# Second attention: the low half of the queries made by VectorE from the PSUM bank, one index copy a batch

## The chip, the core and the metric

The program runs on one NeuronCore of a Trainium2 chip. Its engines are TensorE (PE in the profile, with PEld for its weight loads), VectorE (DVE), ScalarE (ACT), GpSimd (POOL) and SyncE (SP), which here only starts DMAs. Each engine runs its own instructions in the order in which they were written and waits on semaphores. The metric is the device time of one launch in microseconds (us). Three runs of the kernel before took 2513.68, 2516.06 and 2517.75 us, median 2516.06.

## The reference, cut to what matters

The model is a cross attention, a mixture of experts, a second cross attention and a feed-forward layer, for 16 batches of 256 tokens of width 256. The change touches the second attention (16 heads of 64) and the gather of the expert results that stands ahead of it.

```
x = x + tanh(g_ffn[0]) * _L0_ffn_ref(_layernorm(x), ...)          # two experts a token, plus a shared one
x = x + tanh(g_xattn[1]) * _L1_xattn_ref(_layernorm(x), ctx, ctx, mask, ...)

q = split_heads(Q @ W_q + b_q)                                     # Q = _layernorm(x)
k = split_heads(K @ W_k + b_k)                                     # K = V = ctx
v = split_heads(V @ W_v + b_v)
scores = einsum('bhqd,bhkd->bhqk', q, k) / sqrt(d)                 # d = 64
scores = where(mask == 0, -1e9, scores)
probs = softmax(scores, axis=-1)
out = einsum('bhqk,bhkd->bhqd', probs, v)
return out.reshape(...) @ W_o + b_o
```

## The kernel before, in words

The second attention is the function `attention1`. Every float32 matrix is carried as a high and a low half in float16, and a product is three matmuls (high by high, high by low, low by high). So each projected result has to be split: high = float16(value), low = float16(value - high).

A batch has 16 units; unit u is the pair of heads u // 2 for one half of the query rows. The work is a pipeline over batches, written as 16 turns a batch. In a turn TensorE computes the scores of unit u (L1023 to L1027, into one of two banks `pS`), transposes the probabilities of unit u - 3 (L1035), in each even turn multiplies a pair of heads by the values (L1048) and projects an older pair (L1060), and then computes a piece of the next batch's front. VectorE in a turn takes the negative row maximum of the scores (L1212), the inverse of the row sums of unit u - 1 (L1216), the low half of the transposed probabilities (L1222), in even turns the low half of the output (L1227), and then its share of the next batch's front. ScalarE in a turn makes the high half of the transposed probabilities (L1121), in even turns the high half of the output (L1126), then the two exponentials (L1112), then its share of the front. GpSimd in a turn scales the probabilities of unit u - 1 by the inverse sums (L941, "normalise"), then its share of the front, then a gather.

The front of the next batch has three stretches, given by the lists KEYS, QUERIES and VALUES: key chunks on TensorE in turns 2 to 6, query chunks in turns 7, 8, 8, 9, 10, 10, 11, 12, value chunks in turns 12 to 17 (16 and 17 are turns 0 and 1 of the step after). Two banks `pF` serve them in rotation; a chunk waits until the bank's reader two chunks earlier is done. Before the change the path of the four query chunks is: TensorE fills a bank, ScalarE writes the value with bias and the factor 1/8 as float32 to `q32` (L1094, turns 8, 9, 10, 12) and thereby frees the bank, GpSimd casts it to float16 (L923) and subtracts (L925), SyncE starts the DMAs that stack the halves into `QS` (L878, L879), which the scores of the next batch read. Keys go the same way, except that VectorE (L1198) writes the float32 value. Value chunks are read by ScalarE (L1103) and then VectorE (L1205), straight from the bank.

The combine step (`comb`) works two batches ahead: in turns 1, 3, 7 and 11 GpSimd copies a column of row numbers into a small tile (L898) and starts an indirect DMA that gathers 128 rows (L901); in turns 4, 6, 10 and 13 VectorE adds the gathered rows to X (L1153), after every second one it takes row statistics (L1157). GpSimd computes the inverse root (L907), VectorE refines it (L1170 to L1173), and the result `rstd` scales the normalised input `xn` (L1183), which only the queries use.

Of the kernel before, what the change touches and what calls it, by code (L numbers as in the profile page):

```python
# [10 lines left out]
U32 = mybir.dt.uint32  # L11
# [724 lines left out]
def attention1(nc, ctx, X, XW, ctxT_d, mask_d, bias_d, consts, POS, GW, y_d):  # L736
# [7 lines left out]
    UNITS = 2 * PAIRS  # L744
    LIFT = 4096.0
    MASKED = -2.0 ** 40
    QS = [[s.sb(f"QS{i}{a}", [P, PAIRS, S], F16) for a in range(2)] for i in range(2)]
# [14 lines left out]
    maskq = [s.sb(f"maskq{i}", [P, 2, S], BF16) for i in range(2)]  # L762
    k32, q32 = [s.sb(f"k32{i}", [P, 2, S]) for i in range(2)], [s.sb(f"q32{i}", [P, 2, S]) for i in range(2)]
    QN, KN = [s.sb(f"QN{i}", [P, PAIRS, S], F16) for i in range(2)], [s.sb(f"KN{i}", [P, PAIRS, S], F16) for i in range(2)]
# [5 lines left out]
    proj = s.sb("proj", [P, 2, D])  # L770
    pick = [[s.sb(f"pick{i}{q}", [P, 1], U32) for q in range(2 * TOPK)] for i in range(2)]
    routed = [[s.sb(f"routed{i}{q}", [P, D]) for q in range(2 * TOPK)] for i in range(2)]
# [15 lines left out]
    f_full = s.counter("f_full", 13)  # L788
    pick_ready, gathered = s.counter("pick_ready", 4), [[s.counter(f"gathered{i}{q}", 16, start=0) for q in range(4)] for i in range(2)]
    combined, var_ready, root_ready = s.counter("combined", 4), s.counter("var_ready", 1), s.counter("root_ready", 1)  # L790
    comb_steps = s.chain("comb_steps", 7)
    k_flat, q_flat = s.counter("k_flat", 4), s.counter("q_flat", 4)
    qk_high, qk_split = s.counter("qk_high", 8), s.counter("qk_split", 8)
    stacked = [s.counter(f"stacked{half}", 160) for half in range(2)]
# [55 lines left out]
    with nc.Block() as block:  # L850
        @block.sync
        def _(sp):
# [7 lines left out]
            def stack(b, par):  # L860
# [4 lines left out]
                for half in range(2):  # L865
                    qk_split.wait(sp, b, 2 * half + 2)
                    pr = slice(4 * half, 4 * half + 4)
                    for a in range(2):
                        r = slice(64 * a, 64 * a + 64)
                        sp.dma_start(KD2[par][a][0:64, pr, :], KN[0][r, pr, :]).then_inc(stacked[half].sem, 16)  # L870
                        sp.dma_start(KD2[par][a][64:P, pr, :], KN[0][r, pr, :]).then_inc(stacked[half].sem, 16)
                        sp.dma_start(KZ[par][a][0:64, pr, :], KN[1][r, pr, :]).then_inc(stacked[half].sem, 16)
                for half in range(2):
                    qk_split.wait(sp, b, 4 + 2 * half + 2)
                    pr = slice(4 * half, 4 * half + 4)
# [10 lines left out]
        def _(pool):  # L886
# [6 lines left out]
            def comb(b, par, turn):  # L893
                def gather(q):
                    j, k = q // TOPK, q % TOPK
                    if not isinstance(b, int) or b > 1:
                        combined.wait(pool, b, q - 2 * TOPK * 2 + 1)
                    nc.gpsimd.tensor_copy(pick[par][q][:], POS[:, k, bass.ds(2 * b + j, 1)]).then_inc(pick_ready.sem, 1)  # L898
                    pick_ready.wait(pool, b, q + 1)
                    nc.gpsimd.nop(nofuse=True)  # L900
                    nc.gpsimd.indirect_dma_start(out=routed[par][q][:], out_offset=None, in_=y_d,  # L901
                                                 in_offset=bass.IndirectOffsetOnAxis(ap=pick[par][q][:], axis=0)).then_inc(gathered[par][q].sem, 16)

# [6 lines left out]
            def front(b, par):  # L910
# [3 lines left out]

                def split(n):

                    q = n % 4
                    pr = slice(2 * q, 2 * q + 2)
                    dst, src, flat = ((KN, k32, k_flat), (QN, q32, q_flat))[n // 4]
                    flat.wait(pool, b, q + 1)  # L920
                    stacked[q // 2].wait(pool, b, 0)
                    nc.gpsimd.nop(nofuse=True)
                    nc.gpsimd.tensor_copy(dst[0][:, pr, :], src[q % 2][:]).then_inc(qk_high.sem, 1)  # L923
                    qk_high.wait(pool, b, n + 1)
                    nc.gpsimd.tensor_tensor(dst[1][:, pr, :], src[q % 2][:], dst[0][:, pr, :], ALU.subtract).then_inc(qk_split.sem, 1)  # L925

                def make_mask():
# [4 lines left out]
                return plan((0, context_low), (MASK, make_mask),  # L932
                            *[(KEYS[2 * q + 1], lambda q=q: split(q)) for q in range(4)],
                            *[(QUERIES[2 * q + 1], lambda q=q: split(4 + q)) for q in range(4)])

# [11 lines left out]
        def _(pe):  # L947
# [10 lines left out]
            def front(b, par):  # L958
# [29 lines left out]
                def queries(q, a):  # L988
                    if a == 0:
                        if q < 2:  # L990
                            k_flat.wait(pe, b, 3 + q)
                        else:
                            q_flat.wait(pe, b, q - 1)
                    chunk(5 + q, Wv["q"], xh, xl, q, a)

                def values(n, kt):
                    j, half = n // 2, n % 2
                    if kt == 0:
                        if n < 2:
                            q_flat.wait(pe, b, 3 + n)  # L1000
                        else:
# [69 lines left out]
        def _(act):  # L1071
# [5 lines left out]
            def front(b, par):  # L1077
# [55 lines left out]
        def _(dve):  # L1133
# [7 lines left out]
            def comb(b, par, turn):  # L1141
# [35 lines left out]
            def front(b, par):  # L1177
# [14 lines left out]
                def keys(q):  # L1192

                    f_full.wait(dve, b, 2 + q)
                    qk_split.wait(dve, b, q - 1 if q > 1 else -4) if q > 1 or not isinstance(b, int) or b else None
                    for a in range(2):
                        p2 = 2 * q + a
                        last = nc.vector.tensor_scalar(k32[q % 2][:, a, :], pF[(1 + q + par) % 2][:, a * S:(a + 1) * S], bqk[:, 1, p2:p2 + 1], None, ALU.add)  # L1198
                    last.then_inc(k_flat.sem, 1)

                def values(n):
# [1067 lines left out]
```

## Time and profile before

| what | value |
|---|---|
| median of three runs | 2516.06 us |
| the profiled execution, own time | 2506.78 us |
| its span, first to last instruction | 2504.8 us |
| span of the second attention | about 1418 to 2300 us of it |
| one batch of it in the steady state | 52.0 us (L1183 at 1516.36, 1568.36) |
| mean granted clock of TensorE, whole span | 0.916 |

Times are microseconds; "idle before" is the time in which the engine had nothing to run before an instruction, with what ended it. A name such as `a_pT` is a tile of an attention with its buffer number left out. The rows with a time ahead give start, duration, engine, line, operation, output and inputs, and in brackets the idle time before it. An instruction can overlap the tail of the one ahead of it on its engine.

### The profile page before, as it was taken

To read this page: it belongs to the slowest core of one execution; us is meant where nothing else is said; L and a number is where in the kernel's file an instruction comes from. 1 tells how busy PE (TensorE), PEld (TensorE's weight loads), DVE (VectorE), ACT (ScalarE), POOL (GpSimd) and SP (SyncE) were. 2 spreads that over 40 slices of the span, in tenths; PEclk is the share of its full clock that TensorE was granted. 3 is DMA by queue.
4 is the path that set the end of the run, shared out by engine and by line. 5 is a ranking of instruction groups with operands and counts; after the bars stand their busy time and mean duration, and the time that the engine had idled before them with its cause. 6 is when DMAs were issued, how large, how long until landed. Compare 5 with 4: busy or idle time off the path is not lost. (4 is left out here: it accounts for less than half of the span.)

```text
span 2504.8 us, 48924 instructions
## 1 busy us (share of the span) xinstructions
PE 1948.7 (78%) x14975; PEld 1386.5 (55%) x14984; DVE 1609.6 (64%) x3340; ACT 1111.6 (44%) x2557; POOL 876.2 (35%) x1363
## 2 busy tenths in 40 slices
PE   1798988988904597099999679898998889994275
PEld 1576676766603364066666456676666667673122
DVE  5777777877567543044444357777777777776797
ACT  1354444544434122022222146666666666673363
POOL 2000000000000243322332377777776777762004
PEclk9899999999955799599999899999999999997598
DMA  3000000000043000012221133223222232321001
GB/s 101 9 5 8 8 4 8 8 4 4 1 160 128 7 0 1 25 54 66 70 73 57 47 97 79 61 64 83 74 71 70 62 75 74 75 56 36 0 0 67
DMA packets 91507, 118.61 MB, mean 47 GB/s; under 512 B 18264, under 2 KB 60904, under 8 KB 91368
## 3 DMA queue, kind: packets, MB, share of 16 engines
q1 hardware_dynamic: 80872, 94.74, 13.8%
q0 software_dynamic: 8576, 17.87, 2.7%
q10 hardware_dynamic: 1920, 4.19, 0.5%
q8 instruction: 81, 1.33, 0.2%
q14 instruction: 58, 0.48, 0.1%
HBM read 56.92 MB, written 17.90 MB: 30 GB/s over the span
## 5 line engine op out<-in xcount | busy, mean ns | idle before, releaser
L1112 ACT ACTIVATE a_P<-a_pS,a_NM 128x256 f32<-128x256 f32 x512 | 237.2, 470 | 158.1 <-DVE a_NM L1212 157.8
L941 POOL TENSOR_SCALAR a_P<-a_P,a_RS 128x256 f32<-128x256 f32 x512 | 255.3, 499 | 113.2 <-DVE a_RS L1216 75.6
L504 PE MATMUL a_pT<-a_Q,a_K 128*128 128x256 f32 x1024 | 243.0, 383 | 8.6 <-ACT a_PT L587 8.6
L1212 DVE TENSOR_REDUCE a_NM<-a_pS 128x2 f32<-128x512 f32 x256 | 175.5, 686 | 96.6 <-PE a_pS L1027 95.0
L587 ACT ACTIVATE a_PT<-a_pT 128x512 f32<-128x512 f32 x256 | 151.2, 597 | 187.5 <-PE a_pT L504 187.1
L420 POOL TENSOR_TENSOR a_cl<-a_ctxin,a_ch 128x512 f16<-128x512 f32 x16 | 18.6, 1160 | 542.5 <-ACT a_ch L557 542.5
L504 PEld LDWEIGHTS a_pT<-a_Q,a_K 128*128 128x128 f32 x1024 | 183.6, 190 | 38.8 <-ACT a_PT L587 16.5
L1222 DVE TENSOR_TENSOR a_PL<-a_pT,a_PH 128x512 f16<-128x512 f32 x256 | 173.6, 678 | 48.2 <-ACT a_PH L1121 48.0
L1121 ACT ACTIVATE a_PH<-a_pT 128x512 f16<-128x512 f32 x256 | 153.1, 598 | 110.0 <-PE a_pT L1035 95.5
L1035 PE MATMUL a_pT<-g_ident,a_P 128*128 128x128 f32 x1024 | 157.9, 277 | 43.8 <-POOL a_P L941 34.8
L694 DVE TENSOR_REDUCE a_M<-a_pS 128x2 f32<-128x512 f32 x256 | 162.8, 682 | 32.8 <-PE a_pS L483 32.2
L1035 PEld LDWEIGHTS a_pT<-g_ident,a_P 128*128 128x128 f32 x1024 | 117.4, 141 | 74.9 <-POOL a_P L941 52.4
L1027 PE MATMUL a_pS<-a_KZ,a_QS 128*128 128x256 f16 x512 | 125.9, 273 | 0.0
L1026 PE MATMUL a_pS<-a_KD,a_QS 128*128 128x256 f16 x512 | 125.8, 273 | 0.0
L1707 ACT ACTIVATE me_hh<-me_pH 128x512 f16<-128x512 f32 x72 | 43.0, 597 | 175.7 <-PE me_pH L1692 175.7
L99 PE MATMUL a_pF<-a_ch,xw_XW 128*128 128x256 f16 x512 | 98.3, 276 | 27.2 <-DVE a_VL L1205 23.1
L1756 DVE TENSOR_TENSOR me_h<-me_SG,me_pU 128x512 f32<-128x512 f32 x72 | 49.5, 687 | 98.5 <-PE me_pU L99 98.5
L1705 ACT ACTIVATE me_SG<-me_pG 128x512 f32<-128x512 f32 x72 | 43.0, 597 | 147.8 <-PE me_pG L99 147.8
L99 PE MATMUL me_pG<-mo_w1h,me_xt 128*128 x288 | 98.7, 384 | 6.9 <-issue 6.9
L1112 ACT ACTIVATION_READ_ACCUMULATOR a_P<-a_pS,a_NM 128x1 f32 x512 | 102.8, 201 | 0.0
L99 PE MATMUL a_pF<-a_xh,xw_XW 128*128 128x256 f16 x512 | 98.9, 273 | 2.4 <-DVE a_k L1198 2.4
L1023 PE MATMUL a_pS<-a_maskq,g_identb 128*128 128x512 bf16 x256 | 97.4, 380 | 2.9 <-POOL a_maskq L931 2.4
(410 smaller groups left out, 5507.5 us busy)
## 6 DMA issues: line engine op xcount, KB each, us to landing
a_KD<-a_KN SPq DMA_DIRECT2D x128, 128.0 KB
a_QS<-a_QN SPq DMA_DIRECT2D x128, 128.0 KB
we_stage<-mw SPq DMA_DIRECT2D x24, 512.0 KB, 4.7
ys<-me_yb SPq DMA_DIRECT2D x72, 128.0 KB, 1.7
a_ctxin<-ctxT SPq DMA_DIRECT2D x32, 256.0 KB, 2.8
a_KZ<-a_KN SPq DMA_DIRECT2D x64, 128.0 KB
g_X<-x SPq DMA_DIRECT2D x1, 4096.0 KB, 15.0
rows<-mr_row SPq DMA_DIRECT2D x32, 128.0 KB, 1.7
```

The source lines that it names most:

```text
L99: last = nc.tensor.matmul(out, a(kt), b(kt), start=(n == 0), stop=(n == 3 * chunks - 1))
L504: last = nc.tensor.matmul(pT[h % 2][:, kt, :], K32[par][h % 2][:, h // 2, kt * P:(kt + 1) * P], Q32[par][:, h // 2, :], start=True, stop=True)
L587: nc.scalar.activation(PT[h % 8][:], pT[h % 2][:], ACT.Exp, scale=float(dh) ** -0.5).then_inc(p_ready.sem, 1)
L694: nc.vector.reduce_max(M[:, k % 2, k - k % 2:k - k % 2 + 2], pS[k % 2][:], AX.X).then_inc(s_max.sem, 1)
L941: last = nc.gpsimd.tensor_scalar(P32[u % 4][:, a, :], P32[u % 4][:, a, :], RS[u % 4][:, a:a + 1], LIFT, ALU.mult, ALU.mult)
L1026: nc.tensor.matmul(out[:, a, :], q, KD2[par][a][:, p2, :], start=False, stop=False)
L1027: last = nc.tensor.matmul(out[:, a, :], q, KZ[par][a][:, p2, :], start=False, stop=(a == 1))
L1035: last = nc.tensor.transpose(pT[u % 2][:, a, kt, :], P32[u % 4][:, a, kt * P:(kt + 1) * P], ident[:])
L1112: last = nc.scalar.activation(P32[u % 4][:, a, :], pS[u % 2][:, a, :], ACT.Exp, bias=NM[u % 4][:, a:a + 1], accum_out=SM[u % 4][:, a:a + 1])
L1121: nc.scalar.activation(PH[p2 % 2][:, :, :, j * P:(j + 1) * P].rearrange("p a k q -> p (a k) q"), pT[u % 2][:].rearrange("p a k q -> p (a k ...
L1212: nc.vector.tensor_reduce(NM[u % 4][:], pS[u % 2][:], AX.X, ALU.max, negate=True).then_inc(s_max.sem, 1)
L1222: nc.vector.tensor_tensor(PL[p2 % 2][:, :, :, j * P:(j + 1) * P].rearrange(f), pT[u % 2][:].rearrange(f), PH[p2 % 2][:, :, :, j * P:(j + 1 ...
```

## The change

Queries are no longer written as float32. ScalarE reads the bank and writes the float16 high half directly; VectorE then reads the same bank, adds the bias, subtracts the high half and writes the low half; only then is the bank free. GpSimd's cast and subtract remain for the keys alone. The factor 1/8 leaves ScalarE's instruction and goes into the two constants with which `rstd` is refined. The four index copies of a batch become one, into a tile of four columns. The counters that keys and queries shared are parted.

```
     def gather(q):
         ...
-        nc.gpsimd.tensor_copy(pick[par][q][:], POS[:, k, bass.ds(2 * b + j, 1)]).then_inc(pick_ready.sem, 1)
-        pick_ready.wait(pool, b, q + 1)
+        if q == 0:
+            nc.gpsimd.tensor_copy(pick[par][:], POS[:, :, bass.ds(2 * b, 2)]).then_inc(pick_ready.sem, 1)
+            pick_ready.wait(pool, b, 1)
         nc.gpsimd.nop(nofuse=True)
         nc.gpsimd.indirect_dma_start(out=routed[par][q][:], out_offset=None, in_=y_d,
-                                     in_offset=bass.IndirectOffsetOnAxis(ap=pick[par][q][:], axis=0))...
+                                     in_offset=bass.IndirectOffsetOnAxis(ap=pick[par][:, k, j:j + 1], axis=0))...
...
-    def split(n):
-        q = n % 4
+    def split(q):
         pr = slice(2 * q, 2 * q + 2)
-        dst, src, flat = ((KN, k32, k_flat), (QN, q32, q_flat))[n // 4]
-        flat.wait(pool, b, q + 1)
+        k_flat.wait(pool, b, q + 1)
         stacked[q // 2].wait(pool, b, 0)
         nc.gpsimd.nop(nofuse=True)
...
-                *[(QUERIES[2 * q + 1], lambda q=q: split(4 + q)) for q in range(4)])      # GpSimd
...
     def queries(q, a):                                                                    # TensorE
...
-                q_flat.wait(pe, b, q - 1)
+                q_lo.wait(pe, b, q - 1)
...
     def queries(q):                                                                       # ScalarE
         f_full.wait(act, b, 6 + q)
-        qk_split.wait(act, b, 3 + q if q > 1 else 0) if q > 1 or not isinstance(b, int) or b else None
+        stacked[q // 2].wait(act, b, 0)
         for a in range(2):
             p2 = 2 * q + a
-            last = nc.scalar.activation(q32[q % 2][:, a, :], pF[(5 + q + par) % 2][:, a * S:(a + 1) * S], ACT.Identity,
-                                        bias=bqk[:, 0, p2:p2 + 1], scale=float(dh) ** -0.5)
-        last.then_inc(q_flat.sem, 1)
+            last = nc.scalar.activation(QN[0][:, p2, :], pF[(5 + q + par) % 2][:, a * S:(a + 1) * S], ACT.Identity, bias=bqk[:, 0, p2:p2 + 1])
+        last.then_inc(q_hi.sem, 1)
...
+    def queries(q):                                                                       # VectorE
+        q_hi.wait(dve, b, q + 1)
+        for a in range(2):
+            p2 = 2 * q + a
+            last = nc.vector.scalar_tensor_tensor(QN[1][:, p2, :], pF[(5 + q + par) % 2][:, a * S:(a + 1) * S], bqk[:, 0, p2:p2 + 1],
+                                                  QN[0][:, p2, :], ALU.add, ALU.subtract)
+        last.then_inc(q_lo.sem, 1)
...
-        link(nc.vector.tensor_scalar(corr[:], corr[:], -0.5, 1.5, ALU.mult, ALU.add))
+        link(nc.vector.tensor_scalar(corr[:], corr[:], SHRINK * -0.5, SHRINK * 1.5, ALU.mult, ALU.add))    # SHRINK = dh ** -0.5
```

SyncE's wait ahead of the query DMAs is on `q_lo` in place of `qk_split`, TensorE's first two value chunks wait on `q_lo` in place of `q_flat`. No DMA is added or taken away.

On VectorE, turns 8 to 10 of a step before the change (`a1_NM` is written by the maximum, `a1_RS` by the inverse, `a1_PL` by the low half of the probabilities, `a1_ol` by that of the output):

```order
L1212 TENSOR_REDUCE a1_NM0<-a1_pS0 128x2
L1216 RECIPROCAL a1_RS3<-a1_SM3 128x2
L1222 TENSOR_TENSOR a1_PL0<-a1_pT1,a1_PH0 128x4x128
L35 REGISTER_ALU
L1227 SCALAR_TENSOR_TENSOR a1_ol1<-a1_pO,a1_oh1 128x256
L35 REGISTER_ALU
L1212 TENSOR_REDUCE a1_NM1<-a1_pS1 128x2
L1216 RECIPROCAL a1_RS0<-a1_SM0 128x2
L1222 TENSOR_TENSOR a1_PL1<-a1_pT0,a1_PH1 128x4x128
L35 REGISTER_ALU
```

The same place in the changed kernel, where the lines of the maximum, the inverse and the low half are L1218, L1222 and L1228:

```order
L1218 TENSOR_REDUCE a1_NM0<-a1_pS0 128x2
L1222 RECIPROCAL a1_RS3<-a1_SM3 128x2
L1228 TENSOR_TENSOR a1_PL0<-a1_pT1,a1_PH0 128x4x128
L35 REGISTER_ALU
L1233 SCALAR_TENSOR_TENSOR a1_ol1<-a1_pO,a1_oh1 128x256
L1202 SCALAR_TENSOR_TENSOR a1_QN1<-a1_pF1,a1_bqk,a1_QN0 128x256 x2
L35 REGISTER_ALU
L1218 TENSOR_REDUCE a1_NM1<-a1_pS1 128x2
L1222 RECIPROCAL a1_RS0<-a1_SM0 128x2
L1228 TENSOR_TENSOR a1_PL1<-a1_pT0,a1_PH1 128x4x128
L1202 SCALAR_TENSOR_TENSOR a1_QN1<-a1_pF0,a1_bqk,a1_QN0 128x256 x2
```

A pair of instructions on the query bank (L1202) now stands between the work of one turn and the maximum of the turn after it, in turns 8, 9, 10 and 12.

On GpSimd, turns 7 to 10 of a step before the change (`a1_P32` are the probabilities that it normalises):

```order
L898 COPY a1_pick12<-g_POS 128x1
L35 REGISTER_ALU
L901 DMA a1_routed12<-ys,a1_pick12 128x256
L35 REGISTER_ALU
L941 TENSOR_SCALAR a1_P323<-a1_P323,a1_RS3 128x256 x2
L923 CAST a1_QN0<-a1_q320 128x512
L35 REGISTER_ALU
L925 TENSOR_TENSOR a1_QN1<-a1_q320,a1_QN0 128x512
L35 REGISTER_ALU
L941 TENSOR_SCALAR a1_P320<-a1_P320,a1_RS0 128x256 x2
L923 CAST a1_QN0<-a1_q321 128x512
```

The same place in the changed kernel:

```order
L903 DMA a1_routed02<-ys,a1_pick0 128x256
L35 REGISTER_ALU
L940 TENSOR_SCALAR a1_P323<-a1_P323,a1_RS3 128x256 x2
L35 REGISTER_ALU
L940 TENSOR_SCALAR a1_P320<-a1_P320,a1_RS0 128x256 x2
L35 REGISTER_ALU
L940 TENSOR_SCALAR a1_P321<-a1_P321,a1_RS1 128x256 x2
L35 REGISTER_ALU
L940 TENSOR_SCALAR a1_P322<-a1_P322,a1_RS2 128x256 x2
```

The copy ahead of the gather and every cast and subtract between two normalisations are gone from these turns.

## Rows read from the trace of the kernel before

**Rows 1.** One batch: busy us (count) of PE, PEld, DVE, ACT, POOL; clock, DMA share, GB/s.

```profile
1983.00:2035.00 52.00, 47.30 (x414) 35.54 (x413) 38.58 (x87) 33.24 (x103) 39.00 (x60) 1.00 0.29 72
```

**Rows 2.** Waits of TensorE, 1588 to 2185 us: total, times, longest.

```profile
PE a_pT L1035 <- POOL a_P L941: 26.0, 54, 1.8
```

**Rows 3.** TensorE in order of time, one batch: start us, us, instruction [idle before].

```profile
1642.64 0.66 PE L1035 MATMUL a_pT<-g_ident,a_P 128*128 128x128 f32 x4 [0.55 <-POOL a_P L941]
...
1644.44 0.38 PE L1060 MATMUL a_pG<-xw_XW,a_oh 128*128 128x256 f16 x2 [0.36 <-DVE a_proj L1231]
...
1667.96 0.66 PE L1035 MATMUL a_pT<-g_ident,a_P 128*128 128x128 f32 x4 [1.01 <-POOL a_P L941]
...
1678.39 0.28 PE L99 MATMUL a_pF<-a_ch,xw_XW 128*128 128x256 f16 x1 [1.49 <-DVE a_VL L1205]
```

**Rows 4.** GpSimd in order of time, the same batch.

```profile
1640.26 1.16 POOL L925 TENSOR_TENSOR a_KN<-a_k,a_KN 128x512 f16<-128x512 f32 x1
...
1646.18 0.18 POOL L898 COPY a_pick<-g_POS 128x1 uint32 x1
...
1648.26 1.03 POOL L941 TENSOR_SCALAR a_P<-a_P,a_RS 128x256 f32<-128x256 f32 x2
1649.35 0.61 POOL L923 CAST a_QN<-a_q 128x512 f16<-128x512 f32 x1
...
1651.30 1.12 POOL L941 TENSOR_SCALAR a_P<-a_P,a_RS 128x256 f32<-128x256 f32 x2
...
1662.43 1.16 POOL L925 TENSOR_TENSOR a_QN<-a_q,a_QN 128x512 f16<-128x512 f32 x1
```

**Rows 5.** GpSimd, an indirect DMA that follows another, in the expert stage.

```profile
850.84 0.96 POOL L1527 DMA_INDIRECT slots<-st_val,st_idx  x1 [0.30 <-issue]
```

**Rows 6.** VectorE in order of time, the same batch as rows 3.

```profile
1640.62 1.08 DVE L1153 SCALAR_TENSOR_TENSOR g_X<-a_routed,g_GW,g_X 128x256 f32 x1
...
1645.14 0.68 DVE L1212 TENSOR_REDUCE a_NM<-a_pS 128x2 f32<-128x512 f32 x1
...
1646.40 0.41 DVE L1227 SCALAR_TENSOR_TENSOR a_ol<-a_pO,a_oh 128x256 f16<-128x256 f32 x1
...
1651.60 0.47 DVE L1153 SCALAR_TENSOR_TENSOR g_X<-a_routed,g_GW,g_X 128x256 f32 x1
...
1662.77 1.10 DVE L1153 SCALAR_TENSOR_TENSOR g_X<-a_routed,g_GW,g_X 128x256 f32 x1
...
1664.88 0.69 DVE L1212 TENSOR_REDUCE a_NM<-a_pS 128x2 f32<-128x512 f32 x1
...
1667.75 0.68 DVE L1212 TENSOR_REDUCE a_NM<-a_pS 128x2 f32<-128x512 f32 x1
...
1670.85 0.69 DVE L1212 TENSOR_REDUCE a_NM<-a_pS 128x2 f32<-128x512 f32 x1 [0.78 <-PE a_pS L1027]
```

**Rows 7.** ScalarE in order of time, the same batch.

```profile
1643.98 0.59 ACT L1121 ACTIVATE a_PH<-a_pT 128x512 f16<-128x512 f32 x1
1644.46 0.39 ACT L1126 ACTIVATE a_oh<-a_pO 128x256 f16<-128x256 f32 x1
1645.86 0.47 ACT L1112 ACTIVATE a_P<-a_pS,a_NM 128x256 f32<-128x256 f32 x1 [1.00 <-DVE a_NM L1212]
...
1646.77 0.84 ACT L1094 ACTIVATE a_q<-a_pF,a_bqk 128x256 f32<-128x256 f32 x2
...
1661.52 0.60 ACT L1103 ACTIVATE a_VH<-a_pF 128x512 f16<-128x512 f32 x1
```

**Rows 8.** SyncE, the last key DMA of the first batch.

```profile
1450.24 0.60 SPq L872 DMA_DIRECT2D a_KZ<-a_KN  x1
```

**Rows 9.** TensorE, the first scores of the first batch.

```profile
1460.24 0.39 PE L1023 MATMUL a_pS<-a_maskq,g_identb 128*128 128x512 bf16 x1 [2.37 <-POOL a_maskq L931]
```

**Rows 10.** A DMA from HBM: KB each, us from issue to landing.

```profile
a_ctxin<-ctxT SPq DMA_DIRECT2D x32, 256.0 KB, 2.8
```

**Rows 11.** The gathered rows' addition over the whole span: busy, mean ns, idle before.

```profile
L1153 DVE SCALAR_TENSOR_TENSOR g_X<-a_routed,g_GW,g_X 128x256 f32 (+1 forms) x64 | 48.9, 763 | 10.0 <-DMA a_routed<-ys,a_pick 9.6 <-DVE a_bn L1157 0.2
```

More of the change, by code:

```diff
@@ L745, in attention1 @@
     LIFT = 4096.0
+    SHRINK = float(dh) ** -0.5
     MASKED = -2.0 ** 40
@@ L762, in attention1 @@
     maskq = [s.sb(f"maskq{i}", [P, 2, S], BF16) for i in range(2)]
-    k32, q32 = [s.sb(f"k32{i}", [P, 2, S]) for i in range(2)], [s.sb(f"q32{i}", [P, 2, S]) for i in range(2)]
+    k32 = [s.sb(f"k32{i}", [P, 2, S]) for i in range(2)]
     QN, KN = [s.sb(f"QN{i}", [P, PAIRS, S], F16) for i in range(2)], [s.sb(f"KN{i}", [P, PAIRS, S], F16) for i in range(2)]
@@ L770, in attention1 @@
     proj = s.sb("proj", [P, 2, D])
-    pick = [[s.sb(f"pick{i}{q}", [P, 1], U32) for q in range(2 * TOPK)] for i in range(2)]
+    pick = [s.sb(f"pick{i}", [P, TOPK, 2], U32) for i in range(2)]
     routed = [[s.sb(f"routed{i}{q}", [P, D]) for q in range(2 * TOPK)] for i in range(2)]
@@ L788, in attention1 @@
     f_full = s.counter("f_full", 13)
-    pick_ready, gathered = s.counter("pick_ready", 4), [[s.counter(f"gathered{i}{q}", 16, start=0) for q in range(4)] for i in range(2)]
+    pick_ready, gathered = s.counter("pick_ready", 1), [[s.counter(f"gathered{i}{q}", 16, start=0) for q in range(4)] for i in range(2)]
     combined, var_ready, root_ready = s.counter("combined", 4), s.counter("var_ready", 1), s.counter("root_ready", 1)
     comb_steps = s.chain("comb_steps", 7)
-    k_flat, q_flat = s.counter("k_flat", 4), s.counter("q_flat", 4)
-    qk_high, qk_split = s.counter("qk_high", 8), s.counter("qk_split", 8)
+    k_flat, k_high, k_split = s.counter("k_flat", 4), s.counter("k_high", 4), s.counter("k_split", 4)
+    q_hi, q_lo = s.counter("q_hi", 4), s.counter("q_lo", 4)
     stacked = [s.counter(f"stacked{half}", 160) for half in range(2)]
@@ L865, in stack @@
                 for half in range(2):
-                    qk_split.wait(sp, b, 2 * half + 2)
+                    k_split.wait(sp, b, 2 * half + 2)
                     pr = slice(4 * half, 4 * half + 4)
@@ L873, in stack @@
                 for half in range(2):
-                    qk_split.wait(sp, b, 4 + 2 * half + 2)
+                    q_lo.wait(sp, b, 2 * half + 2)
                     pr = slice(4 * half, 4 * half + 4)
@@ L932, in front @@
                 return plan((0, context_low), (MASK, make_mask),
-                            *[(KEYS[2 * q + 1], lambda q=q: split(q)) for q in range(4)],
-                            *[(QUERIES[2 * q + 1], lambda q=q: split(4 + q)) for q in range(4)])
+                            *[(KEYS[2 * q + 1], lambda q=q: split(q)) for q in range(4)])
             def back(b, par):
@@ L999, in values @@
                         if n < 2:
-                            q_flat.wait(pe, b, 3 + n)
+                            q_lo.wait(pe, b, 3 + n)
                         else:
@@ L1194, in keys @@
                     f_full.wait(dve, b, 2 + q)
-                    qk_split.wait(dve, b, q - 1 if q > 1 else -4) if q > 1 or not isinstance(b, int) or b else None
+                    k_split.wait(dve, b, q - 1) if q > 1 or not isinstance(b, int) or b else None
                     for a in range(2):
@@ L1206, in front @@
                 return plan((0, normalised), (START, inputs), *[(KEYS[2 * q + 1], lambda q=q: keys(q)) for q in range(4)],
+                            *[(QUERIES[2 * q + 1], lambda q=q: queries(q)) for q in range(4)],
                             *[(VALUES[2 * q + 1], lambda q=q: values(q)) for q in range(4)])
```

8 lines of the change are left out of this document (4 added, 4 removed).

## Prediction

> **What bounds the kernel now.** I read the stretches first, then the waits of TensorE, then each engine in order of time over one batch of the second attention, the only part that the diff touches. TensorE is busy 47.3 of 52 us at full clock, VectorE 38.6, GpSimd 39.0, ScalarE 33.2 [rows 1]: TensorE sets the pace, and what can be had is its idle time. Its largest wait is for GpSimd's normalise, 26.0 us in the twelve batches of the stretch, 2.2 a batch [rows 2]. In the batch shown there are five of them, from turn 8 to turn 16, the first of 0.55 and the last of 1.01 us; besides them stand 0.36 us for VectorE's read of the projection bank and 1.49 us for VectorE's low half of the values [rows 3]. Why GpSimd is late is seen between two normalises of the query turns: they start at 1648.26 (followed by a cast at 1649.35) and at 1651.30, so a cast and subtract take 1.95 us of a turn that lasts 52 / 16 = 3.25 us [rows 1, 4].
>
> **The change, part by part.** *GpSimd* loses four casts and subtracts, 4 x 1.95 = 7.8 us a batch, all in turns 8 to 12. Of the gathers, one takes 1648.26 - 1646.18 = 2.08 us with its copy [rows 4]; an indirect DMA that has no copy ahead of it takes 0.96 after a gap of 0.30 [rows 5], with 0.07 to the next instruction 1.33. So three gathers lose 0.75 each; bounds are 0.18 (the copy alone) and 1.1 (copy, gap and all). That is 10 us in all, and no normalise of turns 9 to 15 is queued behind anything but its own inverse.
>
> *VectorE* gains eight instructions, 128x256 out of a bank. The nearest rows are 0.41 us (a bank, a float16 operand, a constant) and 0.47 (three operands and a scalar column) [rows 6]. I take 0.47 less the 0.08 that the next one overlaps: 0.78 for a pair, 3.1 us a batch; bounds 0.66 (two of 0.41 with the overlap) and 2.0 (two of 1.10). More than these 3.1 us counts where they stand. The pair waits for ScalarE's high half, which stands behind ScalarE's exponentials, which wait for VectorE's maximum of the same turn. So in turns 8, 9, 10 and 12 the two engines go in lockstep: maximum to exponentials 0.72 (1645.14 to 1645.86), exponentials to high half 0.91 (to 1646.77), high half 0.84 and 0.04 to the release, the pair 0.78, together 3.29 us until the next maximum can start [rows 6, 7]. Behind the waiting pair stand the next maximum, and with it the exponentials, the inverse, the normalise and TensorE's transposes.
>
> I follow this chain from the maximum of turn 8 (1645.14) to that of the next turn 0 (1670.85), 25.71 us before [rows 6]:
> - turns 8 and 9: 3.29 each; turn 10: 3.29 and 0.40 for the gathered rows' addition. 10.27.
> - turn 11 has no pair: maximum, inverse and low half 1.26 (1645.14 to 1646.40).
> - turn 12: ScalarE comes to the exponentials 1.13 after the maximum began (0.72 + 0.91 behind those of turn 11, then 0.48 and 0.28 for the high halves of rows 7, less 1.26), then 0.91, 0.88, 0.78: 3.70.
> - turn 13: 0.72 and 0.91 to the values' high half, 1.25 from there (1661.52) to the addition (1662.77), and from it to the maximum 2.11 before (1664.88), now 1.48: 4.36.
> - turn 14: 0.72 + 0.91 + 1.25 = 2.88.
> - turn 15: from 1667.75 until VectorE is free, 1670.85 - 0.78 = 1670.07: 2.32.
>
> The sum is 24.79, so the next batch begins 0.92 us earlier, and VectorE, not GpSimd, brings it. In turn 13 I took 0.63 off because the addition took 1.10 us beside GpSimd's subtract for queries (1662.43) and 0.47 at 1651.60, beside a normalise [rows 4, 6]; that subtract is gone. The Trainium skill (SBUF — State Buffer, Who interferes with whom) states that a VectorE instruction with two SBUF inputs and a GpSimd instruction that reads SBUF exclude each other, while one with at most one SBUF input does not contend. By that rule the addition beside the subtract was held, and the new pair, with one input in a bank and one in SBUF, is never held by GpSimd; the 1.10 agrees, the 0.47 beside a normalise does not in full. By the rule alone the sum would be the same.
>
> TensorE over the same path: the inverse of turn 14 comes 19.59 + 0.61 after 1645.14, at 1665.34; with an estimated 0.3 to GpSimd and 1.08 for its normalise and the release the transposes of the next turn 0 start near 1666.75, not at 1667.96 [rows 3], 1.2 earlier. TensorE reaches them earlier still, so 1 us of waiting stays, now on VectorE's inverse. Its scores of turn 0 then end near 1669.6, before VectorE is free (1669.93): VectorE's chain is the later one and its 0.92 counts. TensorE's own new wait, on the low half of the queries for a bank, costs nothing: by the same links the bank of the third chunk pair is free at 1648.4 and that of the first value chunk at 1655.0, and in the trace of before TensorE comes to them after 1650 and after 1657, less what it gains.
>
> *Turn 6* gives a second term. The addition at 1640.62 took 1.08 beside the keys' subtract that began at 1640.26 [rows 4, 6]. With the gather of turn 3 shorter by 0.75 the subtract ends at 1640.67; I take 0.45 off (bounds 0 and 0.61). VectorE is what TensorE waits for there (0.36 at 1644.44 [rows 3]), so the maximum of turn 8 and all behind it comes 0.45 earlier; the 0.55 at 1642.64 goes into the same.
>
> A batch: 0.92 + 0.45 = 1.37 us. Fifteen steps have queries beside scores: 20.6 us. *The factor* costs nothing: it sits in two constants of an instruction that is there anyway. ScalarE's instruction is as long with float16 output; the row at 0.60 for 512 and 0.84 for two of 256 leave nothing to fear [rows 7].
>
> *Ahead of the first batch's scores* TensorE waited 2.37 us for the mask, until 1460.24 [rows 9], since the mask on GpSimd stands behind the four query splits. Without them, and with the last two gathers 0.75 shorter, the mask is done some 8 us earlier (4 x 1.95 less what overlaps, and 1.5). What is late next is SyncE: it issues key DMAs until 1450.84 [rows 8], then four for queries at about 0.6 each, the last at 1452.65, and with 2.8 us to land, as for another DMA of this kernel [rows 10], the scores start at about 1455.9. The query halves are there in time, about 1447.4 for these. That is 4.3 us; bounds 1.7 (the DMAs alone move up from 1454.34 to 1452.65) and 8.
>
> The sum is 20.6 + 4.3 = 24.9 us. The profiled execution took 2506.78 us, 2 more than its span and 9.3 less than the median of the runs; so I expect a profiled time near 2481.9 and a median of 2516.06 - 24.9 = 2491.2.
>
> **Rivals.**
> *All of TensorE's waits go* (A): 0.55 + 1.01 and the three between, 2.2 a batch by rows 2 and about 2.5 in the batch shown, with the 0.36 for the bank 2.9; 15 x 2.9 + 4.3 = 48 us, 2468. For it: GpSimd is named as releaser, and VectorE has 13 us a batch free [rows 1]. Against it: its inverse and maximum get the lockstep in their path.
> *The lockstep gives it all back* (B): the four turns cost 0.34 us more each than I count (a longer release from ScalarE, a pair of 0.47 without overlap, a later chunk of TensorE), which is 1.37 a batch. Then only the start is gained, 4 us: 2512.
> *The lockstep costs more* (C), on the slower side: if the new instruction takes the 0.763 us that the addition takes on average over the span [rows 11], a pair is 1.43, 0.65 more than counted; four of them 2.6 a batch, against 1.37 won, so 1.23 lost, 18.5 in fifteen, less 4.3: 14 slower, 2530. It decides from 0.34 + 4.3 / 60 = 0.41 us more in each of the four turns. Against it: the 0.41 of an instruction that also reads a bank and a float16 tile [rows 6].
> *The copies bring nothing* (D): the gap ahead of an indirect DMA is its own. Then turn 6 gives nothing, 15 x 0.92 + 4.3 = 18 us, 2498; it lies inside the forecast's own range.
>
> **How the numbers follow.** The forecast with D, from 2480 to 2506, has 0.60; A 0.14; B 0.12 to 0.13; C 0.13. A measurement of this kernel tells 0.2%, 5 us, from no change. Faster by more than that: 0.60 + 0.14 + 0.02 of B, 0.76; within it 0.12; slower 0.12. The range, 2468 to 2514, reaches to A and B and leaves out C and what lies beyond A. The predicted time is 2491.2.
>
> **What would show it.** In the profile after: TensorE's wait for the normalise a fraction of 26.0 over the same twelve batches, what is left at turn 0 and with VectorE's inverse behind it; the addition of turn 13 near 0.5 us; the new pair at 0.45 to 0.48 an instruction with some 0.9 us of idle time ahead that names ScalarE; the batch at 50.6 us for 52.0; the first scores near 1456. I am wrong if the idle time ahead of maxima names VectorE's own queue no more than before and the batch falls under 50 (A), or if the maxima of turns 9 to 13 come more than 3.6 us apart (B, C).

## The result and the profile after

The changed kernel takes 2490.26 us, median of 4 runs (2489.72 to 2492.03), beside 2516.9 for the kernel before (4 runs, 2513.68 to 2520.81): ratio 0.9895, 95% interval 0.9878 to 0.9912. The forecast was 2491.2. Its profiled execution took 2490.16 us, its span is 2488.2, the mean granted clock 0.911 (0.916 before).

The two profiled executions differ by only 16.6 us. From the first normalised x (L1183 at 1431.84 before, L1180 at 1437.25 after) to the last projection read by VectorE (L1231 at 2284.18, now L1237 at 2263.12) the second attention took 852.3 us before and 825.9 after, 26.5 less. Ahead of it stand 5.4 us more, which arise in the expert stage, and behind it 4.5 us more; the change touches neither (in the traces of the other kernels below the first normalised x stands at 1429.3 to 1433.1), and the execution of before that was profiled took 2506.78 us, 10 us less than the median of 2516.9.

One batch after, in the form of [rows 1] (us, then busy us and count of PE, PEld, DVE, ACT, POOL; clock, DMA share, GB/s):

```profile
1620.16:1670.63 50.47, 46.61 (x412) 35.76 (x412) 39.91 (x94) 32.60 (x103) 31.34 (x49) 1.00 0.30 74
```

52.0 became 50.47; GpSimd has 7.7 us less to do, VectorE 1.3 more. TensorE's busy time fell as well, from 47.30 to 46.61 us, so that its idle time went from 4.70 to 3.86; the ends of its matmuls are modelled, and why the busy time fell is not shown.

This is the shorter of two kinds of batch. The loop has two batches to a pass, and from one pass to the next a batch takes longer, in every kernel of this study: 52.8 to 54.6 us before, 51.5 to 52.8 after. In these two kernels TensorE stands still for 1.8 to 2.6 us there, at the transposes of turn 0, and ScalarE waits for nothing that the profile shows (2.82 us until 1618.90 before). In the changed kernel TensorE's granted clock then falls to the lower of its two levels (1.2 GHz) for 3.5 us, in four of these five places; in the kernel before it does so in one of five. The second of the four, with duration, busy times and clock:

```profile
1712.90:1716.40 3.50, 3.50 (x24) 2.16 (x20) 1.47 (x7) 1.70 (x6) 0.96 (x2) 0.51 0.01 3
```

TensorE's waits over eleven batches (1588 to 2165), beside [rows 2]:

```profile
PE a_pF L99 <- DVE a_VL L1210: 18.5, 11, 2.1
PE a_pT L1034 <- POOL a_P L940: 17.2, 10, 2.4
```

The wait for the normalise fell from 54 times to 10, but in total only from 26.0 to 17.2 us: one long wait a batch stands in place of some five short ones, and about half of the 17.2 us are the longer waits between two passes. TensorE in order of time shows what is left in one batch, beside [rows 3]:

```profile
1660.98 0.66 PE L1034 MATMUL a_pT<-g_ident,a_P 128*128 128x128 f32 x4 [1.43 <-POOL a_P L940]
...
1671.69 0.28 PE L99 MATMUL a_pF<-a_ch,xw_XW 128*128 128x256 f16 x1 [1.77 <-DVE a_VL L1210]
```

VectorE in the same batch, beside [rows 6]; turn 8 begins at 1639.38:

```profile
1635.45 0.48 DVE L1150 SCALAR_TENSOR_TENSOR g_X<-a_routed,g_GW,g_X 128x256 f32 x1
...
1639.38 0.68 DVE L1218 TENSOR_REDUCE a_NM<-a_pS 128x2 f32<-128x512 f32 x1
...
1641.88 0.88 DVE L1202 SCALAR_TENSOR_TENSOR a_QN<-a_pF,a_bqk,a_QN 128x256 f16<-128x256 f32 x2 [0.82 <-ACT a_QN L1092]
1642.67 0.68 DVE L1218 TENSOR_REDUCE a_NM<-a_pS 128x2 f32<-128x512 f32 x1
...
1645.96 0.68 DVE L1218 TENSOR_REDUCE a_NM<-a_pS 128x2 f32<-128x512 f32 x1
...
1649.65 0.68 DVE L1218 TENSOR_REDUCE a_NM<-a_pS 128x2 f32<-128x512 f32 x1
...
1657.47 0.48 DVE L1150 SCALAR_TENSOR_TENSOR g_X<-a_routed,g_GW,g_X 128x256 f32 x1
...
1664.16 0.69 DVE L1218 TENSOR_REDUCE a_NM<-a_pS 128x2 f32<-128x512 f32 x1
...
1667.11 1.58 DVE L1180 TENSOR_SCALAR a_xn<-g_X,a_moments,a_rstd 128x256 f32 x2
1668.61 0.68 DVE L1218 TENSOR_REDUCE a_NM<-a_pS 128x2 f32<-128x512 f32 x1
```

The lockstep is there: a maximum, 0.82 us of waiting for ScalarE's high half, the pair, the next maximum 3.29 us after the first. GpSimd in this batch waits in its turn, beside [rows 4]:

```profile
1643.59 1.03 POOL L940 TENSOR_SCALAR a_P<-a_P,a_RS 128x256 f32<-128x256 f32 x2 [0.83 <-DVE a_RS L1222]
1646.88 1.03 POOL L940 TENSOR_SCALAR a_P<-a_P,a_RS 128x256 f32<-128x256 f32 x2 [2.26 <-DVE a_RS L1222]
```

The first scores of the first batch, beside [rows 9], wait for the query DMAs and no longer for the mask (23.49 us behind the first normalised x, which on the time axis of before is 1455.3; the prediction has 1455.9):

```profile
1460.74 0.38 PE L1022 MATMUL a_pS<-a_maskq,g_identb 128*128 128x512 bf16 x1 [1.70 <-DMA a_QS<-a_QN]
```

**Where the time went, maximum by maximum.** VectorE takes one maximum a turn, so the distances between them (L1212 before, L1218 after) add up to the batch. The table follows one steady batch of the shorter kind in each kernel, from its turn 8 to turn 0 and on to turn 8 of the next. "8 to 9" is the distance from the maximum of turn 8 to that of turn 9; the kernels of the last four columns are described below.

| us | before | after | copy only | queries only | pair later | pair later, x first |
|---|---|---|---|---|---|---|
| 8 to 9 | 2.12 | 3.29 | 2.12 | 3.29 | 2.12 | 2.11 |
| 9 to 10 | 1.74 | 3.29 | 1.75 | 3.29 | 2.46 | 2.46 |
| 10 to 11 | 4.53 | 3.69 | 3.93 | 3.69 | 3.22 | 3.22 |
| 11 to 12 | 1.75 | 1.26 | 1.75 | 1.25 | 2.46 | 2.46 |
| 12 to 13 | 4.42 | 3.70 | 4.27 | 3.71 | 3.22 | 3.22 |
| 13 to 14 | 5.18 | 4.35 | 4.56 | 4.35 | 4.55 | 4.56 |
| 14 to 15 | 2.87 | 2.88 | 2.87 | 2.87 | 2.88 | 2.88 |
| 15 to 0 | 3.10 | 2.32 | 3.11 | 2.31 | 2.32 | 2.32 |
| sum, 8 to 0 | 25.71 | 24.78 | 24.36 | 24.76 | 23.23 | 23.23 |
| 0 to 1 | 4.46 | 4.45 | 4.46 | 4.46 | 4.46 | 2.95 |
| 1 to 8 | 21.83 | 21.23 | 21.24 | 21.82 | 21.25 | 21.33 |
| batch | 52.0 | 50.46 | 50.11 | 51.04 | 48.99 | 47.49 |

The last line is the distance between two batches' index copies; the sums of the links agree with it to 0.06. Before to after is 0.93 in turns 8 to 0 and 0.60 in turns 1 to 8.

### The profile page after: what moved, and what is told of

It reads as the page before. It is cut to its first block and busy times, and to the rows that moved or that the text cites. A ratio compares the mean times of both kernels' runs of the same rounds, so it can differ in the third digit from the quotient of the medians.

```text
span 2488.2 us, 48627 instructions
## 1 busy us (share of the span) xinstructions
PE 1946.7 (78%) x14975; PEld 1392.4 (56%) x14984; DVE 1632.4 (66%) x3468; ACT 1102.1 (44%) x2557; POOL 753.3 (30%) x1187
## 5 line engine op out<-in xcount | busy, mean ns | idle before, releaser
L1218 DVE TENSOR_REDUCE a_NM<-a_pS 128x2 f32<-128x512 f32 x256 | 175.0, 684 | 31.6 <-PE a_pS L1026 28.8
L1228 DVE TENSOR_TENSOR a_PL<-a_pT,a_PH 128x512 f16<-128x512 f32 x256 | 172.7, 675 | 13.2 <-ACT a_PH L1118 13.1
```

The lines of the kernel that those rows point to most:

```text
L1218: nc.vector.tensor_reduce(NM[u % 4][:], pS[u % 2][:], AX.X, ALU.max, negate=True).then_inc(s_max.sem, 1)
L1228: nc.vector.tensor_tensor(PL[p2 % 2][:, :, :, j * P:(j + 1) * P].rearrange(f), pT[u % 2][:].rearrange(f), PH[p2 % 2][:, :, :, j * P:(j + 1 ...
```

## The experiments

All ran beside the kernel before on their own chip: 2508.55 us (11 runs) for the first four, 2509.67 (11 runs) for the last four. Ratios are to that. The times expected in the first four are on the scale of the result above (2516.9 us before), so their ratios are to be compared: 0.986 and 0.997 for the two theories of the first run, 0.993 and 0.989 for the second, 1.008 and 0.991 for the third, 0.983 and 0.989 for the fourth.

### One index copy a batch, queries as before

```
# to the kernel before
-                    nc.gpsimd.tensor_copy(pick[par][q][:], POS[:, k, bass.ds(2 * b + j, 1)])...
+                    if q == 0:
+                        nc.gpsimd.tensor_copy(pick[par][:], POS[:, :, bass.ds(2 * b, 2)])...
```

> The kernel before with one index copy a batch; the queries still go through float32 and GpSimd. Theory 1 (GpSimd is late by little in each turn, and each of three gathers gives back 0.75 us ahead of the turns in which TensorE waits for it): most of the five waits of 0.27 to 1.01 us go, and the addition of turn 13 no longer meets GpSimd's subtract; some 2 us a batch, 1.5 to 2 at the start, about 2482 us. Theory 2 (what counts is GpSimd's load, of which the three gathers are 2.25 of 10 us): a quarter of the gain, 0.4 us a batch, about 2509 us.

Measured: 2477.17 us, ratio 0.9885 (0.9865 to 0.9904), batch 50.11, second attention 824.0 us. The copy alone gives as much as the whole change, and a batch is 1.9 us shorter: Theory 1. Its waits on TensorE, 1600 to 2100:

```profile
PE a_pF L99 <- DVE a_VL L1206: 15.0, 10, 1.6
PE a_pT L1036 <- POOL a_P L942: 9.9, 8, 1.8
```

The batch shows how. The turn-8 maximum stands at 1637.15:

```profile
1638.41 1.03 POOL L902 DMA_INDIRECT a_routed<-ys,a_pick  x1 [0.27 <-issue]
1639.51 1.03 POOL L942 TENSOR_SCALAR a_P<-a_P,a_RS 128x256 f32<-128x256 f32 x2
...
1652.95 1.16 POOL L926 TENSOR_TENSOR a_QN<-a_q,a_QN 128x512 f16<-128x512 f32 x1
```
```profile
1633.16 0.55 DVE L1154 SCALAR_TENSOR_TENSOR g_X<-a_routed,g_GW,g_X 128x256 f32 x1
...
1654.05 0.47 DVE L1154 SCALAR_TENSOR_TENSOR g_X<-a_routed,g_GW,g_X 128x256 f32 x1
```

The normalise behind the gather of turn 7 comes 1639.51 - 1637.15 = 2.36 us after that maximum, before 1648.26 - 1645.14 = 3.12: 0.76 earlier, and the link 10 to 11 is 0.60 shorter. The additions of turns 6 and 13 now start when GpSimd's subtract is all but over (at 1654.05 for one that ends at 1652.95 + 1.16 = 1654.11) and take 0.55 and 0.47 where they took 1.08 and 1.10: the links 13 to 14 and 1 to 8 are 0.62 and 0.59 shorter. With 0.15 in the link 12 to 13 that is all of it, 1.96 by the links and 1.9 by the batches. Against the full change the batch is 0.35 shorter and the first scores come 2.6 us later (26.08 us behind the first normalised x for 23.49), which about cancel: 824.0 and 825.9.

### The queries by VectorE, with four index copies

```
# to the changed kernel
-                    if q == 0:
-                        nc.gpsimd.tensor_copy(pick[par][:], POS[:, :, bass.ds(2 * b, 2)])...
+                    nc.gpsimd.tensor_copy(pick[par][q][:], POS[:, k, bass.ds(2 * b + j, 1)])...
```

> The changed kernel with the four index copies put back. Theory 1 (the chain between VectorE and ScalarE in turns 8 to 15 sets the batch, and the one copy acts only through the addition of turn 6, which meets GpSimd's subtract again): 0.6 us a batch more than the changed kernel, 15 x 0.6 = 9 us, about 2499 us, the batch at 51.1 us. Theory 2 (GpSimd has slack without the query splits, so its copies are free): as the changed kernel, 2490 us.

Measured: 2491.71 us, ratio 0.9929 (0.9914 to 0.9944), batch 51.04, second attention 833.3 us. Ratio and batch are those of Theory 1 (0.993 and 51.1). Turns 8 to 0 last 24.76 us, as in the full change: the copies add nothing there once the queries have left GpSimd. Turn 6 still has its collision. VectorE, and GpSimd beside it:

```profile
1630.67 1.07 DVE L1149 SCALAR_TENSOR_TENSOR g_X<-a_routed,g_GW,g_X 128x256 f32 x1
```
```profile
1630.31 1.16 POOL L924 TENSOR_TENSOR a_KN<-a_k,a_KN 128x512 f16<-128x512 f32 x1
```

So the two parts do not add: alone the copy is worth 1.9 us a batch and the queries 1.0, together 1.54.

### Each instruction of the new pair twice

```
# to the changed kernel, ahead of L1202; spare is a tile that nobody reads
+                        nc.vector.scalar_tensor_tensor(spare[:, p2, :], pF[(5 + q + par) % 2][:, a * S:(a + 1) * S], bqk[:, 0, p2:p2 + 1],
+                                                       QN[0][:, p2, :], ALU.add, ALU.subtract)
```

> The changed kernel with each of VectorE's eight query instructions done a second time, into a tile nobody reads. Theory 1 (lockstep, all of it on the path): each of the four turns grows by 0.78 us, 3.1 a batch, 47 us in fifteen steps, about 2537 us. Theory 2 (VectorE has 10 us a batch to spare and TensorE sets the pace): under 10 us slower, about 2495 us.

Measured: 2537.58 us, ratio 1.0111 (1.0097 to 1.0126), batch 54.7, that is 4.2 more than after, where 4 x 0.78 = 3.1 stand in the chain. Two maxima and what is between them:

```profile
1646.95 0.68 DVE L1221 TENSOR_REDUCE a_NM<-a_pS 128x2 f32<-128x512 f32 x1
...
1649.44 0.48 DVE L1203 SCALAR_TENSOR_TENSOR a_spare<-a_pF,a_bqk,a_QN 128x256 f16<-128x256 f32 x1 [0.82 <-issue]
1649.84 0.48 DVE L1205 SCALAR_TENSOR_TENSOR a_QN<-a_pF,a_bqk,a_QN 128x256 f16<-128x256 f32 x1
...
1651.02 0.68 DVE L1221 TENSOR_REDUCE a_NM<-a_pS 128x2 f32<-128x512 f32 x1
```

The link is 4.07 for 3.29, by 0.78 longer: the pair lies in the path with its full length, as the prediction has it. The other 1.1 us stand in one link, from turn 15 to 0: 3.4 to 3.6 us for 2.32. TensorE waits 2.49 us for the transposes of turn 0 (1.43 in after), and then its clock is granted at the lower level, so that the scores of the next turn 0 come late and VectorE waits for them:

```profile
1671.66 0.66 PE L1035 MATMUL a_pT<-g_ident,a_P 128*128 128x128 f32 x4 [2.49 <-POOL a_P L941]
```
```profile
1672.80:1676.40 3.60, 3.60 (x20) 1.97 (x16) 2.26 (x8) 1.78 (x6) 0.96 (x2) 0.53 0.00 0
```
```profile
1675.94 0.69 DVE L1221 TENSOR_REDUCE a_NM<-a_pS 128x2 f32<-128x512 f32 x1 [1.24 <-PE a_pS L1027]
```

The trace has the comparison in itself. In the first batch of each of the loop's six passes TensorE has this wait. In the last of them (2070.99 to 2124.58) the clock stays at full speed behind the same 2.49 us; the link is 2.32 and the batch 53.59, that is 3.1 more than after. So the doubled pair costs its own length, and beyond that, in five of these six batches, what a longer wait of TensorE brings with it.

### VectorE's query pairs one turn later

```
# to the changed kernel
-                            *[(QUERIES[2 * q + 1], lambda q=q: queries(q)) for q in range(4)],
+                            *[(QUERIES[2 * q + 1] + 1, lambda q=q: queries(q)) for q in range(4)],
```

> The changed kernel with VectorE's query pairs one turn later, behind the maximum, the inverse and the low halves of that turn, so that they no longer wait for ScalarE. Theory 1 (the idle time of 0.8 to 1.2 us ahead of each pair is on the path of the batch): four such waits go, TensorE's wait at turn 0 (1.43 us) goes with them, and the batch falls by about 1 us until TensorE bounds it: about 2475 us. Theory 2 (the pair's own 0.78 us are what counts, not where they stand): 2490 us.

Measured: 2462.2 us, ratio 0.9806 (0.9790 to 0.9821), batch 48.99, second attention 806.3 us. A turn later ScalarE's high half is done when VectorE comes to it: no idle time is left ahead of the pair, and turns 8 to 0 take 23.23 us for 24.78. TensorE's wait for the normalise at turn 0 (1.43 us in the batch shown of after) is gone, and the batch is 1.47 shorter. A pair in turn 9, without idle time ahead of it:

```profile
1635.31 0.69 DVE L1228 TENSOR_TENSOR a_PL<-a_pT,a_PH 128x512 f16<-128x512 f32 x1 [0.30 <-ACT a_PH L1118]
1635.92 0.87 DVE L1202 SCALAR_TENSOR_TENSOR a_QN<-a_pF,a_bqk,a_QN 128x256 f16<-128x256 f32 x2
1636.70 0.68 DVE L1218 TENSOR_REDUCE a_NM<-a_pS 128x2 f32<-128x512 f32 x1
```

What TensorE still waits for, 1600 to 2100:

```profile
PE a_pF L99 <- DVE a_VL L1210: 17.3, 10, 1.8
```

### x normalised a turn ahead

In each of the kernels so far the link 0 to 1 takes 4.46 us; in it stands the pair L1180 (1.58 us in after, beside GpSimd's subtract of the class biases, L915 at 1667.07 for 1.15). The batch of this pair is two batches ahead of the one that is scored, and its inverse deviation is ready well before.

```
# to the kernel of the last section; in plan() of the scores' step, ahead of the values' halves
+                                *([(UNITS, lambda: normalised(b + 2, par))] if not isinstance(b, int) or b + 2 < B else []))
# and in the front's plan, only the first two batches keep it
-                return plan((0, normalised), (START, inputs), ...
+                return plan(*([(0, lambda: normalised(b, par))] if isinstance(b, int) and b < 2 else []), (START, inputs), ...
```

> The changed kernel with VectorE's query pairs one turn later (batch 48.98 us, ratio 0.981 in the run of that alone), and with the two instructions that normalise x for the projections of batch b+2 (L1180) written by VectorE in turn 0 of the step, ahead of the values' halves, where it otherwise waits for ScalarE; they now stand at the head of the next step, beside GpSimd's subtract of the class biases. T3 (what TensorE waits for once the pairs are out of the way is this pair: 1.58 us for two beside GpSimd's subtract, 0.73 when nothing runs beside it): its instructions take 0.36 us each, the largest wait left on TensorE at turn 0 (1.78 us for VectorE's low half of the values) falls by about 1.4, the batch to 47.6 us, ratio about 0.972. Rival T4 (that wait is the length of the lockstep between ScalarE and VectorE at the values' halves, and the pair only fills time in which VectorE is idle anyway): batch and ratio as without the move, 49.0 us and 0.981.

Measured: 2445.87 us, ratio 0.9743 (0.9727 to 0.9759), batch 47.49, second attention 786.3 us. T3 holds, T4 falls. The ratio is a little above the 0.972 expected, though the batch (47.49) and the attention (20.0 us less than without the move) are as expected; the profiled execution of this kernel took 2439.47, the lowest of its five (the other four 2445.5 to 2446.7). VectorE in turn 0:

```profile
1650.85 0.69 DVE L1219 TENSOR_REDUCE a_NM<-a_pS 128x2 f32<-128x512 f32 x1
...
1652.44 0.83 DVE L1179 TENSOR_SCALAR a_xn<-g_X,a_moments,a_rstd 128x256 f32 x2
1653.20 0.69 DVE L1211 TENSOR_TENSOR a_VL<-a_pF,a_VH 128x512 f16<-128x512 f32 x1
1653.80 0.68 DVE L1219 TENSOR_REDUCE a_NM<-a_pS 128x2 f32<-128x512 f32 x1
```

And without the move, in the kernel with the later pairs:

```profile
1655.35 0.69 DVE L1218 TENSOR_REDUCE a_NM<-a_pS 128x2 f32<-128x512 f32 x1
...
1657.70 0.69 DVE L1210 TENSOR_TENSOR a_VL<-a_pF,a_VH 128x512 f16<-128x512 f32 x1 [0.67 <-ACT a_VH L1100]
1658.30 1.59 DVE L1180 TENSOR_SCALAR a_xn<-g_X,a_moments,a_rstd 128x256 f32 x2
1659.81 0.68 DVE L1218 TENSOR_REDUCE a_NM<-a_pS 128x2 f32<-128x512 f32 x1
```

In both the low half of the values starts 2.35 us after the maximum (1653.20 - 1650.85, 1657.70 - 1655.35). So the moved pair costs nothing where it now is, it fills the wait for ScalarE; and where it was, the 1.51 us between the end of the low half and the maximum are gone. TensorE's wait for that low half falls from 17.3 us to this, and the batch is at 47.49 with TensorE busy 46.81 of it:

```profile
PE a_pF L99 <- DVE a_VL L1211: 2.4, 8, 0.4
```
```profile
1608.62:1656.11 47.49, 46.81 (x417) 36.04 (x415) 39.27 (x94) 32.98 (x103) 31.52 (x48) 1.00 0.32 79
```

That holds for the shorter kind of batch. The batches between two passes of the loop take 48.9 to 49.1 us, and the largest wait that TensorE has left is the one there, without a releaser that the profile names:

```profile
PE a_pT L1034 <- issue: 7.7, 5, 1.7
```

### The copy and x first, queries left on GpSimd

The edits of the first and the last section together, on the kernel before.

> The kernel before with the one index copy a batch (which alone gave 0.9885 and a batch of 50.11 us) and the pair that normalises x moved as in later_xn_first; GpSimd still splits the low halves of the queries. T3: 1.4 us a batch less, 48.7 us, ratio about 0.980. T4: 50.1 us and 0.9885. It also tells whether the query part of the change is worth anything in the best version: if this one is within 0.2% of later_xn_first, it is not; I expect it 0.8% longer, since GpSimd's normalise is still waited for.

Measured: 2464.46 us, ratio 0.9806 (0.9787 to 0.9824), batch 48.62, 1.49 less than with the copy alone: the same gain as on the other kernel. Against the version with the later pairs it is 1.13 us a batch and 0.6% of the whole longer. That is what the query part of the change is worth, once its pair is out of the lockstep; 0.8% was expected.

### The factor left in ScalarE's instruction

```
# to the changed kernel
+                                                    scale=SHRINK)
-                    link(nc.vector.tensor_scalar(corr[:], corr[:], SHRINK * -0.5, SHRINK * 1.5, ALU.mult, ALU.add))
+                    link(nc.vector.tensor_scalar(corr[:], corr[:], -0.5, 1.5, ALU.mult, ALU.add))
```

> The changed kernel with the factor 1/8 back in ScalarE's query instruction (scale of the activation) and the constants of x's inverse deviation as before; VectorE's subtract then takes the bank without the factor, so its low half is not that of the reference (its length is the same). The prediction has the factor at nothing: the same time as the changed kernel, within 0.1%, ScalarE's instruction of 256 columns at its 0.45 us. Rival: a scale beside a bias makes ScalarE's instruction longer by 0.05 us or more, which in four turns in lockstep gives 0.2 us a batch, 3 us.

Measured: 2483.55 us, ratio 0.9897 (0.9877 to 0.9916), batch 50.46. This kernel leaves the factor out of VectorE's subtract, so its low halves are not those of the model; the instructions are as many and as long. The factor costs and brings nothing: the ratio is that of the changed kernel beside it (0.9893, the next run), and ScalarE's query instruction takes 0.48 us in both.

### The changed kernel again

> The changed kernel itself, run beside the three below, so that they are compared with it on one chip. All theories: a ratio to the kernel before of 0.9895, with the batch of the second attention at 50.5 us.

Measured: 2484.45 us, ratio 0.9893 (0.9873 to 0.9913), batch 50.56, second attention 825.6 us.

## Why the prediction was right, point by point

- **The bound.** TensorE sets the pace of the batch and what is had is its idle time. In the shorter batches at full clock its busy time is 47.3 us before, 46.6 after, 46.6 with the later pairs and 46.4 to 46.8 in the fastest kernel, and the batch comes down to 47.49 as its waits go: 1.47 us with the 1.43 at the transposes, 1.50 with the 1.6 to 1.8 at the values' bank.
- **The chain from turn 8 to turn 0**: predicted 24.79, measured 24.78. Its links were 3.29, 3.29, 3.69, 1.26, 3.70, 4.36, 2.88 and 2.32; measured 3.29, 3.29, 3.69, 1.26, 3.70, 4.35, 2.88, 2.32. The pair was priced at 0.78; two of them with the overlap take it to 0.79 (1641.88 to 1642.67). Rival C, a pair of 1.43, is out; the doubled pair, which lengthens each link by all of its 0.78, shows that C's price per link was right and its duration wrong.
- **What is left at turn 0.** The transposes were put 1666.75 - 1645.14 = 21.61 us behind the turn-8 maximum; they come 1660.98 - 1639.38 = 21.60 behind it. The wait there is 1.43 us, predicted 1. Rival A, that all waits go, fails on it, and the run with the later pairs shows that nothing but the place of the pair kept A from being so for this wait.
- **Turn 6: the mis-sized term.** Predicted 0.45 (bounds 0 to 0.61); measured 0.60 by the turns 1 to 8, and 0.58 between the runs with four copies and with one (51.04 - 50.46). The prediction had the subtract end 0.05 us after the addition starts and left 0.15 us of the loss in place for such an overlap. In after the subtract (1634.47 for 1.16 us) overlaps the addition (1635.45) by 0.18 and nothing of the loss is left. Over the fourteen steps that have this addition the difference is 2.1 us.
- **The start.** Predicted 4.3 us earlier; from the first L1183 or L1180 to the first scores 28.40 us before and 23.49 after, 4.9 earlier, and to the first maximum 5.7 earlier. The limiter is the one named, the query DMAs.
- **The sum.** The attention is 26.5 us shorter: 5.7 until the first maximum, where 4.3 was predicted, and 20.8 in the steps, where 20.6 was. That the second pair of numbers agrees so well is in part luck, for the fifteen steps are not alike, as the prediction took them to be. Twelve of them save 16.6 together and not 12 x 1.53 = 18.4, since 2 us are lost again between the passes of the loop, where the changed kernel's clock falls more often (four stretches of 3.5 us for one). The first step saves 2.4 and the one behind the loop 1.8. The last of the fifteen saves nothing: it has no gathers and no additions, and takes 47.78 us in both kernels. Against that, turn 6 gives more than was counted. The medians differ by 26.6, near the attention's 26.5 though the profiled executions differ by 16.6; with runs of the kernel before from 2513.68 to 2520.81 that is no check to the microsecond. On the other chip the medians of the changed kernel and the one before differ by 25.2.
- **Whose gain it is.** The prediction gave 0.92 of the 1.37 us to VectorE's query halves and 0.45 to the copies. For the step from the one to the other, queries first and copies after, this is what the runs show (0.96 and 0.58). It is not what each is worth: the copies alone bring 1.9, more than both. The prediction read the kernel before as made late by GpSimd's four casts and subtracts. Of that lateness 1.9 us a batch go with three copies: 0.76 us ahead of one normalise, and two collisions with an addition. The casts and subtracts cost 1.13 us a batch more, as the two kernels with x first show, and the lockstep of the new pairs takes that back: turns 8 to 0 last 24.78 us in the changed kernel and 24.36 with the copy alone. Rival D had the copies at nothing, and it is wrong in either order.

The collision itself has a plain form in these runs: the addition ends 0.28 us after GpSimd's subtract, or after its own 0.48 us if that is later. Starts of the addition 0.36, 0.34, 0.36, 0.27 and 0.89 us into a subtract of 1.16 us gave 1.08, 1.10 [rows 4, 6], 1.07, 1.18 (queries only) and 0.55 us (copy only); 1.16 - 0.36 + 0.28 = 1.08, and so on for each. Who begins first matters: at 1482.95 in the kernel before an addition starts 0.06 us ahead of a subtract and takes 0.47, and the subtract takes 1.43 for 1.16. By the Trainium skill (SBUF — State Buffer, Who interferes with whom) a VectorE instruction with two SBUF inputs contends with a GpSimd instruction that reads SBUF. The traces agree for the GpSimd subtract, which has two inputs. For GpSimd instructions with one input they mostly do not: the addition at 1657.47 takes 0.48 wholly beside the mask (L931, 1656.65 for 1.94). But in the first batch, at 1458.20 before and 1455.12 with the copy alone, where a mask begins within 0.03 us of an addition, the addition takes 0.93 and 0.91; no run separates this case.

## What to carry to other kernels

A wait named for a busy engine is not yet a reason to take work off it: ask by how much it is late, and try the smallest thing that removes so much. Where two engines hand over twice within one turn, put the second hand-over a turn later before counting instructions. And look at what the other instructions do in the turn in which the pace-setting engine waits: one that has long been ready may stand there, and fill another wait for nothing elsewhere. Here these two moves made the fastest version of the study, 2445.87 us, ratio 0.9743, where the change itself has 0.9895.

## What the runs showed of the hardware that was not expected

- The pair that normalises x, float32 from one SBUF tile to another, takes 0.73 us alone, 0.83 when a normalise ends beside it, and 1.58 to 1.59 beside GpSimd's subtract of two tiles (1.15 us). It has one tile as input. The same section of the Trainium skill names tensor_scalar among the operations that can use both of VectorE's SBUF ports and then contend with GpSimd. The prediction's sentence on instructions with one SBUF input leaves that out; for its new pair, which has one input in a bank and one in SBUF, nothing hangs on it. The traces agree with the section: in after only the first of the two is held, 1.26 us from 1667.11, until 0.15 us behind the end of the subtract (1667.07 for 1.15), and the second takes 0.40. No run tried the pair by itself; all agree on the lengths.
- An indirect DMA on GpSimd starts 0.27 us after the instruction ahead of it when its index tile has long been written, and 0.77 to 0.82 after the copy that writes it. So a copy of 0.18 us costs about 0.7.
- A scale beside a bias in ScalarE's instruction costs nothing: the batch is 50.46 with it and without.
- A wait of TensorE can cost more than its length. With the doubled pair TensorE waits 2.48 or 2.49 us in the first batch of each of the loop's six passes; behind five of these waits the clock is granted at the lower level for 3.5 us and the link from turn 15 to 0 is 3.4 to 3.6 us, behind the sixth it is not and the link is 2.32.
